# Banded attention: scores of both token halves in shared PSUM columns, and value products of 34 weights

## What is computed

```python
OFFSETS = sorted(set(range(33)) | {48, 64, 96, 128, 192, 256, 384})
qkv = x @ Wqkv + bqkv                      # 16 heads of 16
scores = stack([einsum('bhnd,bhnd->bhn', q, shift(k, delta)) for delta in OFFSETS]) * scale + pos_bias
alpha = softmax(scores over OFFSETS)       # keys before the first token are masked
out = sum(alpha[..., i] * shift(v, OFFSETS[i]))
flat * sigmoid(x @ Wgate + bgate) @ Wout + bout
```

## Time and profile before

| | |
|---|---|
| runs | 3433.63, 3435.17, 3417.03 us; median 3433.63 |
| span of the profiled execution | 3413.9 us |
| TensorE busy, share | 2844.6 us, 83% |
| VectorE, ScalarE, GpSimd | 48%, 42%, 24% |
| matmul instructions | 45724 |
| banded attention | about 0 to 1383 us of the span |
| score, maxima and value-product matmuls of the banded stage (L582, L587, L665, L675) | 28928 instructions |

### The profile page before, as it was taken

How to read it: one execution, slowest core, us unless ns; L and a number is a source line. 1 busy time by engine, 2 the same in 40 slices (tenths; PEclk the granted TensorE clock), 3 DMA queues, 4 the chain that set the end, 5 groups by cost and what they waited for, 6 DMA issues and landing times. The chain is left out here.

```text
span 3413.9 us, 101201 instructions
## 1 busy us (share of the span) xinstructions
PE 2844.6 (83%) x45724; PEld 1618.9 (47%) x45724; DVE 1633.9 (48%) x2745; ACT 1439.6 (42%) x1425; POOL 811.5 (24%) x567
## 2 busy tenths in 40 slices
PE   2678888978888886799569899998989899997897
PEld 1455565656556565434334444444444444443444
DVE  2444343344344443600666666666666666663401
ACT  1454444444534443410235454555545554554401
POOL 3343433343434331000412122222222221210002
PEclk9789898889889897899679999999999999998998
DMA  6332323243333331388042122222222221221397
GB/s 182 87 101 66 95 66 97 70 107 77 94 79 80 82 93 36 115 326 365 19 92 58 44 57 55 57 57 57 57 57 57 56 58 40 56 39 58 152 420 268
DMA packets 233548, 344.23 MB, mean 101 GB/s; under 512 B 113691, under 2 KB 142181, under 8 KB 216741
## 3 DMA queue, kind: packets, MB, share of 16 engines
q1 hardware_dynamic: 207892, 310.02, 31.2%
q10 hardware_dynamic: 25232, 27.83, 3.4%
HBM read 266.15 MB, written 69.24 MB: 98 GB/s over the span
## 5 line engine op out<-in xcount | busy, mean ns | idle before, releaser
L1362 DVE TENSOR_REDUCE b_tops<-b_slot 128x8 f32<-128x1024 f32 x576 | 680.1, 1219 | 358.1 <-PE b_slot L1217 180.6
L1403 ACT ACTIVATE b_probs<-b_slot 128x1024 f32<-128x1024 f32 x576 | 583.0, 1023 | 550.7 <-PE b_slot L1217 396.3
L512 POOL COPY a_q_far<-a_q_near 96x1024 bf16<-96x1024 bf16 x128 | 259.1, 2054 | 344.4 <-PE a_slot L587 218.6
L1164 POOL TENSOR_SCALAR_AFFINE_SELECT b_probs<-b_probs 128x1024 f32<-128x1024 f32 x128 | 139.8, 1093 | 808.1 <-ACT b_probs L1403 808.1
L1237 PE MATMUL b_outT_ps<-b_probs,b_v 128*17 128x128 f32 (+3 forms) x4608 | 319.4, 385 | 6.2 <-ACT b_probs L1403 5.6
L1217 PE MATMUL b_slot<-b_q_stack,b_k_stack 99*128 99x512 bf16 (+3 forms) x1280 | 275.6, 322 | 43.5 <-DVE b_tops L1362 32.8
L888 ACT ACTIVATE a_k_far<-a_k_near 96x1024 bf16<-96x1024 bf16 x128 | 258.3, 2068 | 102.7 <-DMA a_k_near<-parts_near_dram 93.6
L1217 PE MATMUL b_slot<-b_k_stack,b_q_stack 96*128 96x512 bf16 (+3 forms) x1280 | 266.7, 323 | 29.4 <-DVE b_tops L1362 20.6
L788 DVE TENSOR_TENSOR a_probs<-a_slot,a_bias_k 128x1024 f32<-128x1024 f32 x128 | 154.4, 1217 | 182.9 <-PE a_slot L587 182.7
L797 DVE TENSOR_REDUCE a_tops<-a_slot 128x16 f32<-128x1024 f32 x128 | 156.3, 1221 | 135.9 <-PE a_slot L587 134.9
L851 ACT ACTIVATE a_probs<-a_probs 128x1024 f32<-128x1024 f32 x128 | 133.3, 1053 | 176.3 <-DVE a_probs L788 153.8
(11 more groups left out here) (226 smaller groups left out, 4262.0 us busy)
## 6 DMA issues: line engine op xcount, KB each, us to landing
f_w_ring<-in_L_ffn_w_dram SPq DMA_DIRECT2D x128, 1024.0 KB, 9.9
parts_near_dram<-a_parts ACTq DMA_DIRECT2D x96, 256.0 KB
parts_dram<-b_parts SPq DMA_DIRECT2D x96, 256.0 KB
a_k_near<-parts_near_dram SPq DMA_DIRECT2D x128, 128.0 KB, 3.0
b_k_stack<-parts_dram SPq DMA_DIRECT2D x64, 256.0 KB, 6.8
a_q_near<-parts_near_dram SPq DMA_DIRECT2D x64, 192.0 KB, 2.9
b_q_stack<-parts_dram SPq DMA_DIRECT2D x32, 384.0 KB, 4.5
values_dram<-a_v_stage SPq DMA_DIRECT2D x16, 544.0 KB, 3.8
```

The lines of the kernel that those rows point to most:

```text
L512: pool.tensor_copy(q_far[far][0:QK_ROWS, h, :].rearrange("p (r a) -> p r a", r=LINKS), q_near[near][0:QK_ROWS, h, :].rearrange("p (a r) -> ...
L1362: ins = dve.tensor_reduce(out, src, AX.X, ALU.max)
L1403: act.activation(probs_of(b, g, u, h)[:, :], slot_of(step)[:, :], ACT.Exp).then_inc(taken_act, 1)
```

## The change

Scores. `products` is split. `maxima` is its half for `mx`, with the same instructions. `scores` is new: for each of 16 column blocks s of 32 queries it writes two matmuls, one for the query block s (PSUM rows 0 to 63) and one for the block s + 16 in the other half of the tokens (rows 64 to 127), each with 64 keys (the block before and its own) as weights and 32 queries as columns. Far scores likewise: 64 keys of a residue as weights, the first 32 queries into rows 0 to 63, the other 32 into rows 64 to 127. That is 65 matmuls a set where there were 48.

Values. `v_near` and `v_far` hold, for each column block, two copies of the group's values (f): one for the first token half in rows 0 to 63, one for the other in rows 64 to 127, with zeros in the other rows. One matmul has 34 weights: 17 for each half. It takes 32 columns. Near and far together are 128 matmuls a head group (256 instructions) where there were 260 (520). Heads write rows 0 or 64 and one of the two PSUM banks. In the weights the head is now the innermost index, so that the 34 weights of a head lie 4 fp32 apart in one run; `v_stage` and the values in DRAM have the same order. `vin` issues 5 loads in place of 6, with overlapping rows.

Around it: the bias for the scores (`bias_k`) has 32 columns in place of 64, `ot` transposes in another order and divides in two halves of half the size, and `std` shares `rstd`'s memory.

```diff
-        v_stage = sb("v_stage", [P, 4, H, HD + 1])
+        v_stage = sb("v_stage", [P, 4 * G, HD + 1, HG])
         VW = HG * (HD + 1)
-        v_near = sb("v_near", [P, NT, 4, VW])
-        v_far = sb("v_far", [P, LINKS, VW])
+        V_ENTRIES = 2 * (COLS + LINKS)
+        v_home = sb("v_home", [P, V_ENTRIES * VW])
+        v_near = v_home[:, 0:2 * COLS * VW].rearrange("p (s f d) -> p s f d", f=2, d=VW)
+        v_far = v_home[:, 2 * COLS * VW:V_ENTRIES * VW].rearrange("p (r f d) -> p r f d", f=2, d=VW)
...
-                        for c in range(4):
-                            sp.dma_start(v_near[BLK * c:BLK * (c + 1), :, c, :],
-                                         src.rearrange("(i c p) d -> c p i d", c=4, p=BLK)[c]).then_inc(v_in, 16)
-                        for r2 in range(2):
-                            sp.dma_start(v_far[RES * r2:RES * (r2 + 1), r2:LINKS:2, :],
-                                         src.rearrange("(a r c) d -> c a r d", c=2, r=NT)[r2]).then_inc(v_in, 16)
+                        line = H * (HD + 1)
+
+                        def windows(first, rows, blocks):
+                            return bass.AP(src.tensor, src.offset + first * line, [[line, rows], [BLK * line, blocks], [1, VW]])
+
+                        sp.dma_start(v_near[0:2 * BLK, 1:COLS, 0, :], windows(0, 2 * BLK, COLS - 1)).then_inc(v_in, 16)
+                        sp.dma_start(v_near[BLK:2 * BLK, 0, 0, :], src[0:BLK, :]).then_inc(v_in, 16)
+                        sp.dma_start(v_near[2 * BLK:4 * BLK, :, 1, :], windows(N // 2 - BLK, 2 * BLK, COLS)).then_inc(v_in, 16)
+                        by_residue = src.rearrange("(a r) d -> a r d", r=LINKS)
+                        sp.dma_start(v_far[0:RES // 2, :, 0, :], by_residue[0:RES // 2]).then_inc(v_in, 16)
+                        sp.dma_start(v_far[RES:2 * RES, :, 1, :], by_residue).then_inc(v_in, 16)
...
-                def products(dst, rows, h, left, right, ahead, start):
-
-                    for blk in range(N // BLK):
+                def maxima(dst, h, q, k):
+
+                    for blk in range(QBLKS):
                         i, c = divmod(blk, 4)
-                        lo = BLK * blk - (0 if ahead else BLK)
-                        first, last = max(lo, 0), min(lo + 64, N)
-                        at = 64 * i - lo
-                        pe.matmul(dst[BLK * c:BLK * (c + 1), at + first:at + last], left[0][rows, h, BLK * blk:BLK * (blk + 1)],
-                                  right[0][rows, h, first:last], start=start, stop=True, skip_group_check=True)
+                        lo = BLK * blk - BLK
+                        first = max(lo, 0)
+                        at = 64 * i + first - lo
+                        pe.matmul(dst[BLK * c:BLK * (c + 1), at:64 * i + 64], q[0][0:QK_ROWS, h, BLK * blk:BLK * (blk + 1)],
+                                  k[0][0:QK_ROWS, h, first:lo + 64], start=False, stop=True, skip_group_check=True)
                     for r in range(LINKS):
                         pair, r2 = divmod(r, 2)
                         at = 512 + 64 * pair
-                        ins = pe.matmul(dst[RES * r2:RES * (r2 + 1), at:at + 64], left[1][rows, h, RES * r:RES * (r + 1)],
-                                        right[1][rows, h, RES * r:RES * (r + 1)], start=start, stop=True, skip_group_check=True)
+                        ins = pe.matmul(dst[RES * r2:RES * (r2 + 1), at:at + 64], q[1][0:QK_ROWS, h, RES * r:RES * (r + 1)],
+                                        k[1][0:QK_ROWS, h, RES * r:RES * (r + 1)], start=False, stop=True, skip_group_check=True)
+                    return ins
+
+                def scores(dst, h, q, k):
+
+                    def near(row, at, keys, queries):
+                        pe.matmul(dst[row:row + keys.stop - keys.start, at:at + BLK], k[0][0:ALL_ROWS, h, keys], q[0][0:ALL_ROWS, h, queries],
+                                  start=True, stop=True, skip_group_check=True)
+
+                    block = lambda j, n=1: slice(BLK * j, BLK * (j + n))
+                    near(BLK, 0, block(0), block(0))
+                    near(0, 0, block(QBLKS - 2), block(QBLKS - 1))
+                    for s in range(COLS):
+                        for half in range(2):
+                            j = s + COLS * half
+                            if j:
+                                near(2 * BLK * half, BLK * s, block(j - 1, 2), block(j))
+                    for r in range(LINKS):
+                        for half in range(2):
+                            at = 512 + BLK * r
+                            first = RES * r + BLK * half
+                            ins = pe.matmul(dst[RES * half:RES * (half + 1), at:at + BLK], k[1][0:ALL_ROWS, h, RES * r:RES * (r + 1)],
+                                            q[1][0:ALL_ROWS, h, first:first + BLK], start=True, stop=True, skip_group_check=True)
...
-                        if k == 0:
-                            for blk in range(4 * c, 4 * c + 4):
-                                lo, end = BLK * blk, min(N, BLK * blk + 64)
-                                while lo < end:
-                                    top = min(end, (lo // 512 + 1) * 512)
-                                    for h in range(HG):
-                                        at = 64 * c + lo - BLK * blk
-                                        ins = pe.matmul(outT_ps[BLK * h:BLK * h + HD + 1, lo:top],
-                                                        v_near[:, c, blk % 4, (HD + 1) * h:(HD + 1) * (h + 1)],
-                                                        probs[h][:, at:at + top - lo], start=lo in (0, 512) and blk in (0, 15), stop=False,
-                                                        skip_group_check=True)
-                                    lo = top
-                        else:
-                            for r in (2 * c, 2 * c + 1):
-                                for half in range(2):
-                                    for h in range(HG):
-                                        at = 512 + 64 * c + 32 * half
-                                        ins = pe.matmul(outT_ps[BLK * h:BLK * h + HD + 1, 512 * half + r:512 * (half + 1):LINKS],
-                                                        v_far[:, r, (HD + 1) * h:(HD + 1) * (h + 1)],
-                                                        probs[h][:, at:at + 32], start=False, stop=c == NT - 1,
-                                                        skip_group_check=True)
+                        entries = v_far if k else v_near
+                        for s in (2 * c, 2 * c + 1):
+                            for h in range(HG):
+                                pair, row = divmod(h, 2)
+                                lo = 512 * pair
+                                rows = slice(64 * row, 64 * row + 2 * (HD + 1))
+                                to = outT_ps[rows, lo + s:lo + 512:LINKS] if k else outT_ps[rows, lo + BLK * s:lo + BLK * (s + 1)]
+                                both = entries[:, s, :, :].rearrange("p f (d h) -> p h (f d)", h=HG)[:, h, :]
+                                ins = pe.matmul(to, both, probs[h][:, 512 * k + BLK * s:512 * k + BLK * (s + 1)], start=not k and not s,
+                                                stop=bool(k) and c == NT - 1, skip_group_check=True)
...
-                        for i in range(NT):
-                            ins = pe.transpose(dst[:, i * P:(i + 1) * P], outT[:, i * P:(i + 1) * P], ident[:, :])
+                        for i in range(NT // 2):
+                            for pair in range(2):
+                                n, at = 2 * i + pair, 512 * pair + P * i
+                                ins = pe.transpose(dst[:, n * P:(n + 1) * P], outT[:, at:at + P], ident[:, :])
...
-                            ins = dve.tensor_tensor(probs[h][:, :].rearrange("p (k t c) -> p k t c", k=2, c=64),
-                                                    src[:, :].rearrange("p (k t c) -> p k t c", k=2, c=64),
-                                                    bias_k[:, HG * g + h, :, :].unsqueeze(2).to_broadcast([P, 2, NT, 64]), ALU.add)
+                            ins = dve.tensor_tensor(probs[h][:, :].rearrange("p (k t c) -> p k t c", k=2, c=BLK),
+                                                    src[:, :].rearrange("p (k t c) -> p k t c", k=2, c=BLK),
+                                                    bias_k[:, HG * g + h, :, :].unsqueeze(2).to_broadcast([P, 2, COLS, BLK]), ALU.add)
...
-                            dve.reciprocal(recip[:, :, :], o[:, :, :, HD]).then_inc(recip_done, 1)
+                            sums = src[:, :].rearrange("p (n f) -> p n f", f=64)[:, :, HD:2 * (HD + 1):HD + 1]
+                            dve.reciprocal(recip[:, :, :], sums).then_inc(recip_done, 1)
                             dve.wait_ge(recip_done, b * G + g + 1)
```

(17 more changed lines are left out.)

20 lines of the change are left out of this document (9 added, 11 removed).

## The result

| | before | after |
|---|---|---|
| median of the runs | 3429.77 us (4 runs, 3417.03 to 3435.17) | 3506.59 us (4 runs, 3499.51 to 3511.47) |
| span of the profiled execution | 3413.9 us | 3509.8 us |
| ratio, 95% interval | | 1.0237, 1.0199 to 1.0275 |

The change makes the kernel 77 us slower. The forecast was 3474 us: right in direction and inside its range, and about half of the cost in size.

What follows compares the result with a forecast made beforehand. TensorE was taken to bound the banded attention, busy 1041 of 1270 us. Scores 31, value products 6 and VectorE 3 gave +40 us on the 3433.6 us median: 3474 us, range 3370 to 3525 (forecast's own 3440 to 3510).

Steps and rivals of the forecast that it cites:

- rival D: Score stretches: half the columns per matmul lose full clock more often; stage mean 0.83, 50 us more, 3524 us; chance 0.08.
- A score set: Scores, 128 sets: 1.27 us against 0.72 at full clock, 1.98 at half clock; raw cost 84 us.
- How much of the scores is hidden: Scores: all hidden in group 2; two sets of 0.65 us exposed in three groups of four, 31 us.
- The clock: Score sets: a third taken at half clock, from the stage's mean clock of 0.87 before the change.
- The value products: PV, 32 head groups: 34 strided weights at 1.67 ns, 31 ns a product, 7.9 us a group against 6.0.
- the bf16 row: Profile row behind the load pace: 12 bf16 weights 16 bytes apart take 98 ns, 1.67 ns each.
- What the longer products cover: Value products: hide issue stalls 25 and 8 us, maxima's rows 12, chain before L648 10; +6 us left.
- VectorE, value loads: Output product in two halves of at most 0.45 us, 3 us; value loads -2 to +10 us, taken at 0.
- Rival A: Value products: weights at 16 bytes load as fast as together; total -52 us, 3382 us; chance 0.28.
- B: Scores: narrow matmuls not limited by their load; 3448 us, the same within 0.5%; chance 0.12 together with E.
- C: Value products: strided fp32 pays fourfold or two tiles' loads go in turn; 65 ns each, +280, 3750 us; chance 0.07.
- E: Far value products stay issue-limited, the edit does half of what it says; within B's time; chance 0.12 together with B.

Runs made afterwards that it cites:

- The values alone: The changed kernel with the 48 wide score matmuls of the kernel before in place of its 65; 3441.13 us, ratio 1.0053 to the kernel before.
- the value half alone: The changed kernel with the score matmuls of before (last near one at 64 columns) and the 34 weights lying together; 3373.44 us, ratio 0.9850.

## Why the prediction was right in direction and half in size

In the columns of the account the forecast's 40 us (39 by these rounded terms) were: "full" 131 (70 for the scores, 61 for the values), "clock" 13, hidden or gone as waits 108, and 3 for VectorE. The trace has 151, 57 and 112. So the waits were right in sum, "full" was short by 20, and the clock by 44. The time lies 3 us inside the forecast's own range of 3440 to 3510 us. It lies that high because of the clock, the mechanism of rival D with its chance of 0.08, and not because of a term of the sum; that the range still held it is luck.

- **A score set**: 1.27 us at full and 1.98 at half clock were forecast; the timeline above has 1.24 and 1.96. That the load of 64 weights, and not 32 columns, sets the pace is shown by both runs with 64 columns: a set takes 1.24 us there too.
- **How much of the scores is hidden**: two sets a phase in groups 0, 1 and 3, all in group 2. Waits in the score phases fell by 42 us against 53 that the forecast hid (84 less 31), and group 2 stayed near its length (19.65 us against 19.79 in batch 4, 19.2 against 18.8 on average). This step held to some 10 us.
- **The clock: the step that failed.** The sum took a third of the sets at half clock, the share of the trace before, as if it stayed. It rose from 0.33 to 0.42 of the sets and from 0.45 to 0.60 of the maxima's, and the projections came into it: +57 us where the 84 had 13 for it (128/3 x (0.86 - 0.55) us, in the sets alone). Rival D named just this, with a stage mean of 0.83 and a price of 50 us; the trace has 0.82 and 57. The mistake was to keep it as a case apart, at a chance of 0.08. The forecast's own numbers gave reason to price it: about 3000 columns in 0.72 us a set before, about 2100 in 1.27 us after. The run with 64 columns at the same loads then showed it, 46 us less at a stage mean of 0.90.
- **The value products**: forecast 31 ns each at 1.67 ns a weight, load 135 ns, raw +61; measured 34 ns, load 161 ns ((161 - 78)/34 = 2.4 ns a weight), raw +78. The term was mis-sized by 17 us, 12 of them in the near part: between its bounds of 17 and 65 ns, with the bf16 row as a good guide to the order but not to the size. The 16 us that the value products no longer lose to half clock, which the sum doesn't have either, made up for it: luck.
- **What the longer products cover**: 55 us forecast (issue stalls 33, maxima's rows 12, the chain before L648 10). By waits it was 47 + 4 + 4 = 55. The sum is right by luck, the parts aren't: the stalls vanished whole, the other two hardly moved. The values alone cost 18 us against the forecast's 9 with VectorE's part; the 9 to 11 us that the value products start later behind step L680 (below) stand in no term of it.
- **VectorE, value loads**: the two divisions take 0.419 us each against at most 0.45, and the changed kernel waits 2.6 us ahead of the first value products, so the value loads cost nothing there, as forecast. The upper bound of 10 us was real all the same: with the short score sets the wait is 16.7 us.
- **Rival A**, weights at 16 bytes as fast as together, is refuted by 161 against 115 ns. Its time would have been wrong too: the run with the weights together in the changed kernel is A's case, and it took 3452 us, not 3382. Against before it has "full" 24 us up and "waits" some 88 down, near A's terms, but "clock" 105 up. Only the value half alone, with the scores of before, comes out at 3373. B falls by the set of 1.24 us, C by 34 ns, E by the 0.7 us of stalls that are left. The Trainium skill's statement (SBUF — State Buffer, "Door 1: The DMA port swizzle") that one can stride for free up to 4 fp32 or 8 bf16 fits two of the three points here, together and 8 bytes apart, and not the third, 16 bytes: 161 ns. The same passage of the Trainium skill says that full bandwidth needs at least two accesses to a 16-byte line; that fits all three, four and two weights a line at 115 and 114 ns and one at 161. Here the measurement decides; had the sum gone by the free stride of 4 fp32, it would have ended near 3382.

## What to carry over

When a matmul's load sets its pace, cutting its columns saves little or nothing and can let the clock fall, for its neighbours too; price the clock in the forecast itself and not as a side case. Before giving such a shape up, let it take more columns than needed where the surplus is overwritten: 46 us here for a few lines. And have the weights of a short fp32 matmul at most 8 bytes apart, but count the transfers that this takes: here they cost more than they brought.

## What the runs showed that I had not expected

- A strided load doesn't follow the clock. A step of 16 value products takes 0.54 us at full and 0.52 us at half clock (lower quartiles to the next step's start), while a score set goes from 1.24 to 1.96 us. The load itself takes 161 ns at either clock; with the weights together it takes 113 ns at full and 170 ns at half clock. At 16 bytes apart something other than TensorE's clock is the limit.
- 34 fp32 weights take 115 ns together and 114 at 8 bytes apart, and 161 at 16.
- After step L680 (L648 before) the next value products start later: 0.81 us after the step's first matmul at full clock (882.25 in the timeline above, next start 883.05), against 0.47 to 0.52 before. It is so in every kernel here with the 34-weight products and in none with those of before. The 16 matmuls of the step did not get slower: from the first start to the last they take 0.66 us in both kernels. Before, the value products of 17 weights start 0.49 us after the first, before the step's last three; those of 34 weights start 0.15 us after the last. So the step no longer overlaps with what follows. That this comes from the wider shape of the products is likely, since it is all that these kernels share, but no run tests why.
- Faster work can lower the clock: each time the value products got shorter, the stage's mean clock fell (0.82 to 0.78, 0.87 to 0.84, 0.90 to 0.87) and took part of the gain. So the columns of the scores are not the whole account of the clock, and no run here says what else is.
